# A row-number map carried as the 129th float of each gathered row

## What is computed

```python
agg = jax.ops.segment_sum(x[src], dst, num_segments=N_NODES)
h = x + agg
h = jnp.maximum(h @ wa + ba, 0.0)
return h @ wb + bb
```

## Time and profile before

| | us |
|---|---|
| median of 2 runs | 3564.31 |
| lowest and highest of them | 3557.01, 3571.61 |
| span of the profiled execution, first to last instruction | 5308.1 |
| opening, in the profiled execution | 0 to 49.3 |
| dense layers, in it | 49.3 to about 1465 |
| sums of the first layer, in it | about 1465 to 1965 |

### The profile page before, as it was taken

One profiled execution on the slowest core, in us unless ns is written; L12 is line 12 of the kernel. 1 busy time (PEld: TensorE's weight loads), 2 busy tenths in 40 slices (PEclk: granted clock), 3 DMA queues, 4 the chain that ended last, 5 costly groups with the idle time before them and its releaser, 6 DMA issues. The chain is left out here.

```text
span 5308.1 us, 70155 instructions
## 1 busy us (share of the span) xinstructions
PE 3134.5 (59%) x18625; PEld 2527.0 (48%) x18625; DVE 2677.8 (50%) x8976; ACT 2356.1 (44%) x6177; POOL 2154.2 (41%) x2226
## 2 busy tenths in 40 slices
PE   1110107999867779868756403997029970178864
PEld 1000006777644445534446403996029870177764
DVE  1000008999943346559846301775006860199875
ACT  0000007999812224447735302775017750188765
POOL 6777760000045555546366473001740017500366
PEclk7555559999967777779967656987559975598555
DMA  2200004444434433425556423765227752276542
GB/s 77 56 9 8 18 9 140 174 172 170 164 117 127 119 87 108 112 90 168 164 155 200 142 63 104 225 196 163 62 72 233 220 177 61 58 245 232 169 125 82
DMA packets 430539, 673.46 MB, mean 127 GB/s; under 512 B 81411, under 2 KB 168086, under 8 KB 430252
## 3 DMA queue, kind: packets, MB, share of 16 engines
q1 hardware_dynamic: 354764, 558.83, 32.6%
q0 software_dynamic: 70464, 108.96, 8.9%
q10 hardware_dynamic: 5024, 2.30, 0.2%
HBM read 378.46 MB, written 295.50 MB: 127 GB/s over the span
## 5 line engine op out<-in xcount | busy, mean ns | idle before, releaser
L647 POOL DMA_INDIRECT msgs<-t_gat,row_i x600 | 574.3, 957 | 1081.6 <-POOLq L157 895.1
L664 POOL DMA_INDIRECT dg_g_ring<-in_x,dst_i x200 | 192.2, 961 | 860.5 <-DVE g_xb L1222 782.9
L2229 ACT ACTIVATE t_nnt<-t_p_nt,cxt 128x512 f32<-128x512 f32 x294 | 200.4, 682 | 756.0 <-remote 265.3
L1754 PE MATMUL t_p_q<-mean_col,t_nsq 128*128 128x1 f32 x2352 | 332.6, 263 | 273.2 <-issue 243.0
L1754 PEld LDWEIGHTS t_p_q<-mean_col,t_nsq 128*128 128x128 f32 x2352 | 342.9, 224 | 280.8 <-issue 280.8
L2023 POOL DMA_INDIRECT out_rows<-t_x,own_i x200 | 204.4, 1022 | 491.1 <-ACT t_x L2279 437.9
L2109 PE MATMUL t_p_nt<-ident,t_nh 128*128 128x128 f32 x1176 | 217.7, 316 | 309.3 <-issue 176.1
L1747 PE MATMUL t_p_nh<-wx,t_nnt 128*128 128x132 f32 x1568 | 265.1, 320 | 178.9 <-issue 156.1
L800 PE MATMUL de_p_o<-wc,de_hh 128*128 128x128 f32 x1568 | 225.8, 289 | 151.5 <-DVE de_r L948 124.3
L2109 PEld LDWEIGHTS t_p_nt<-ident,t_nh 128*128 128x128 f32 x1176 | 158.1, 163 | 328.9 <-issue 231.4
L1747 PEld LDWEIGHTS t_p_nh<-wx,t_nnt 128*128 128x128 f32 x1568 | 228.4, 221 | 179.9 <-issue 179.4
(11 more groups left out here) (405 smaller groups left out, 9434.7 us busy)
## 6 DMA issues: line engine op xcount, KB each, us to landing
t_nh<-t_gat SPq DMA_DIRECT2D x294, 264.0 KB
t_gat<-t_nhn SPq DMA_DIRECT2D x196, 264.0 KB
t_x<-de_x SPq DMA_DIRECT2D x196, 256.0 KB
t_ah<-t_gat SPq DMA_DIRECT2D x150, 264.0 KB
t_x<-t_x SPq DMA_DIRECT2D x148, 256.0 KB
t_gat<-t_ahn SPq DMA_DIRECT2D x100, 264.0 KB
t_gat<-de_h SPq DMA_DIRECT2D x98, 264.0 KB
de_x<-in_x SPq DMA_DIRECT2D x97, 256.0 KB
```

Source lines behind the costliest of these rows:

```text
L647: self.nc.gpsimd.indirect_dma_start(out=self.msgs[:, c, 0:width], out_offset=None, in_=table, in_offset=bass.IndirectOffsetOnAxis(ap=idx[: ...
L664: nc.gpsimd.indirect_dma_start(out=ring[:, u, j, :], out_offset=None, in_=a["x"], in_offset=bass.IndirectOffsetOnAxis(ap=self.dst_i[:, i * ...
L1754: last = self.nc.tensor.matmul(p_q[:, j:j + 1], sq[:, j * D:(j + 1) * D], self.mean_col[:], start=True, stop=True)
L2229: nc.scalar.activation(nnt[:, g % 2], p_nt[:], ACT.Identity, bias=bias).then_inc(act_nt, 1)
```

## The change

There is no `t_where` any more. A new table `t_xw` in DRAM has NPAD rows of MW = 129 floats: a node's row of `x` and, as 129th float, the number of the row where the node is right. Slot numbers are now held as floats.

- In the opening POOL first writes the nodes' own row numbers (`node_row`, in the memory of `deg`). ACT, after its 26 loads, issues 7 DMAs that write these into the 129th place of every row, 128 x 56 single floats each, and then 16 that copy `x` from DRAM into the 129-float rows, 3125 rows of 512 bytes each. Two semaphores that outlive the block count their landings.
- The opening prepares target numbers (`dst_i`) before source numbers, and the resident gathers into `msgs` now bring target rows. They read `x` as before.
- POOL waits for the fills, scatters the slot numbers (into `t_xw` now), gathers the last LATE = 8 chunks, waits for the copies and the scatters, and then brings source rows of 129 floats through the ring. The reads of the map and the two copies of zeroes are gone.
- In the first layer's sums the ring's rows go to the scan and the resident rows to the addition. DVE copies the 129th floats of each group into `row_i`, one small copy for each of the 50 groups.

```diff
     def load(act):
         for dst, src in loads:
             act.dma_start(dst, src).then_inc(loaded, 16)
+        act.wait_ge(self.nodes_told, 1)
+        t = NPAD // 128
+        rows = self.xw[0:NPAD, D:MW].rearrange("(p t) o -> p (t o)", p=128)
+        for n in range(FILLS):
+            part = slice(n * t // FILLS, (n + 1) * t // FILLS)
+            act.dma_start(rows[:, part], self.node_row[:, part]).then_inc(self.map_filled, 16)
+        for n in range(COPIES):
+            part = slice(n * N // COPIES, (n + 1) * N // COPIES)
+            act.dma_start(self.xw[part, 0:D], a["x"][part, :]).then_inc(self.x_copied, 16)
...
-        self.resident_gather(self.src_i, a["x"], D, got, range(FIRST, CHUNKS))
+        self.resident_gather(self.dst_i, a["x"], D, self.got, range(FIRST, CHUNKS - LATE))
+        pool.wait_ge(self.map_filled, 16 * FILLS)
         for c in range(CHUNKS):
             nc.gpsimd.indirect_dma_start(
-                out=self.where, out_offset=bass.IndirectOffsetOnAxis(ap=self.put_i[:, c:c + 1], axis=0),
+                out=self.places, out_offset=bass.IndirectOffsetOnAxis(ap=self.put_i[:, c:c + 1], axis=0),
                 in_=self.slot_id[:, c:c + 1], in_offset=None).then_inc(mapped, 16)
-        for i in range(UN):
+        self.resident_gather(self.dst_i, a["x"], D, self.got, range(CHUNKS - LATE, CHUNKS))
+        pool.wait_ge(self.x_copied, 16 * COPIES)
+        pool.wait_ge(mapped, 16 * CHUNKS)
+        for i in range(AG):
             rows(i)
-        pool.wait_ge(got, 16 * CHUNKS)
-        for n in range(2):
-            pool.dma_start(self.msgs[0:1, n * ROWP:(n + 1) * ROWP, 0:D],
-                           self.t4[SLOTS:SLOTS + ROWP, :].rearrange("(o c) f -> o c f", o=1)).then_inc(self.zeroed, 16)
-        pool.wait_ge(mapped, 16 * CHUNKS)
-        ahead = CHUNKS - (AG - UN)
-        for c in range(ahead):
-            look(c)
-        for i in range(UN, AG):
-            rows(i)
-            look(ahead + i - UN)
-        pool.wait_ge(self.map_taken, 16 * CHUNKS)
...
+                    if live(k, u, 1, AG):
+                        dve.wait_ge(arrived[v], 16 * G4 * (k + (0 if u < 1 else 1)))
+                        nc.vector.tensor_copy(self.row_i[:, bass.ds((i - 1) * G4, G4)], xs[:, v, :, D]).then_inc(s["dve_row"], 1)
```

More of the change, by code:

```diff
@@ L35 @@
 XW = D + 4
+MW = D + 1
+COPIES = 16
+FILLS = 7
 RE = 2 * CE
@@ L178, in allocate @@
         self.got = ctx.enter_context(nc.semaphore("got"))
+        self.x_copied = ctx.enter_context(nc.semaphore("x_copied"))
+        self.map_filled = ctx.enter_context(nc.semaphore("map_filled"))
         def sb(name, shape, dt=F32):
@@ L315, in store @@
             sp.dma_start(self.t4[SLOTS:SLOTS + 128, :], spread[:, 3, :]).then_inc(stored, 16)
+            for n in range(N, NPAD, 128):
+                m = min(NPAD, n + 128)
+                sp.dma_start(self.xw[n:m, 0:D], spread[0:m - n, 3, :]).then_inc(stored, 16)
             sp.wait_ge(loaded, 16 * len(loads))
-            sp.wait_ge(stored, 16)
+            sp.wait_ge(stored, 48)
         def fill(pool):
+            nc.gpsimd.iota(self.node_row, pattern=[[1, NPAD // 128]], base=SLOTS, channel_multiplier=NPAD // 128,
+                           allow_small_or_imprecise_dtypes=True).then_inc(self.nodes_told, 1)
             nc.gpsimd.memset(self.ident[:], 0.0).then_inc(ready, 1)
@@ L416, in turn @@
             last.then_inc(columns, 1)
-        return load, store, fill, fold, turn, stored, ready
+        return load, store, fill, fold, turn, ready
     def segments_parts(self, sb, ps, sem):
@@ L451, in segments_parts, with store @@
                                 a[name][whole * RE:E].rearrange("(o k) -> o k", o=1)))
[L452 to L455, removed]
+        dst_loaded, dst_row, dst_turned, dst_ready = (sem(n) for n in ("dst_loaded", "dst_row", "dst_turned", "dst_ready"))
+        n_loads = len(other_loads) + 1
         def load(sp):
             sp.wait_ge(cleared, 4)
-            for dst, src in src_loads:
-                sp.dma_start(dst, src).then_inc(src_loaded, 16)
-            for dst, src in dst_loads + other_loads:
+            for dst, src in dst_loads:
+                sp.dma_start(dst, src).then_inc(dst_loaded, 16)
+            for dst, src in other_loads:
                 sp.dma_start(dst, src).then_inc(loaded, 16)
             sp.dma_start(wcomp[:], a["L1_gnn_w_comp"].rearrange("(o r) b -> o r b", o=1).to_broadcast([128, 8, 4])).then_inc(loaded, 16)
[L465 to L469, removed]
+        def store(sp):
+            sp.wait_ge(told, 7)
+            sp.dma_start(self.unplaced, self.slot_id[:]).then_inc(gone, 16)
             sp.wait_ge(flagged, 1)
@@ L505, in find @@
             of = lambda n: p[n][:, 0:CHUNKS].rearrange("q (j p) -> q j p", j=2)
-            dve.wait_ge(src_loaded, 32)
+            dve.wait_ge(dst_loaded, 16 * len(dst_loads))
             dve.wait_ge(cleared, 4)
[L508 to L511, removed]
+            after(nc.vector.tensor_copy(dstf[:], dst_raw[:]))
+            cur = halves(dstf[:, 1:RE + 1])
+            nc.vector.tensor_scalar(halves(row[:, 1])[:, :, 1:128], cur, float(N - 1), None, ALU.min).then_inc(dst_row, 1)
+            dve.wait_ge(dst_turned, 1)
+            nc.vector.tensor_copy(both(self.dst_i[:]), of(1)).then_inc(dst_ready, 1)
             dve.wait_ge(loaded, 16 * n_loads)
-            dve.wait_ge(told, 8)
-            after(nc.vector.tensor_copy(dstf[:], dst_raw[:]))
+            dve.wait_ge(told, 7)
             after(nc.vector.memset(dstf[0:1, 0:1], -1.0))
-            cur = halves(dstf[:, 1:RE + 1])
             at = lambda t: halves(t[:])[:, :, 1:128]
@@ L583, in turn @@
             idp = self.ident[0:ROWP, 0:ROWP]
-            for n in range(1, 6):
+            for n in (0, 2, 3, 4, 5):
                 for j in range(2):
```

99 lines of the change are left out of this document (50 added, 49 removed).

## The result

The changed kernel takes 3804.02 us (two runs, 3798.41 and 3809.64), before it was 3564.31: a ratio of 1.0688, 95% interval 1.0644 to 1.0733, or +239.7 us. The forecast was 3880, in a range of 3480 to 4040. The profiled execution of the changed kernel is one of the timed ones: its own time is 3809.64 us, its span 3807.8.

A forecast was written before the change was run, and what follows sets the result against it. Dense work, bounded by DVE, and POOL's queue were taken to reach the sums almost together, with POOL setting the sums' pace. +376 us (opening) and -60 (sums) on 3564.3 gave 3880 us, range 3480 to 4040.

The forecast's parts named there:

- Dense work beside POOL: Ahead of the sums: in timed runs dense work goes on beside POOL at its own pace, 6.85 us a group.
- ACT is held until its queue has drained: In the opening: 100,176 pieces hold ACT, so the next block begins at 425 us instead of 49.3, +376 us.
- Five engines for 3125 rows: In the opening: each 3125-row copy runs on 5 engines, its largest divisor up to 16; 149 rows a us.
- Drain of the fills: On ACT's queue in the opening: 50,176 pieces of 4 bytes drain in 75 us, between 38 and 105.
- Drain of the copies: On ACT's queue in the opening: 50,000 rows of 512 bytes drain in 335 us, between 263 and 750.
- the sum: Whole kernel: +376 us in the opening and -60 in the sums, +316 on 3564.3, giving 3880 us.
- Rival 2: In the opening: ACT held, but copies use 16 engines and take 105 us; total 3650 us; chance 0.10.
- POOL perhaps 30 us later: Ahead of the sums: dense work ends near 760 us, POOL near 790; removing 154 reads saves at most 30 us.
- -60 us for the reads: In the sums: removing the reads of the map saves 60 us, between 0 and 93.
- POOL's pace of 6.3 us a group: In the sums: POOL needs 290 us, 6.3 us a group, and PE is near that pace as well.
- The 50 small copies on DVE: In the sums: copies of about 171 ns each, 8.6 us in all, hidden beside DVE's other work.

The follow-up runs named there:

- e9: The kernel before plus only 16 copies of x on ACT's queue, 3136-row pieces, into a plain unread 128-float table, no fills: 3628.82 us in one execution.
- e3: The kernel before with the change's fills and copies added on ACT's queue, into a table nobody reads: 5659.94 us against 5330.86, ratio 1.0596.
- e11: The changed kernel with its copies issued by SP as 98 pieces beside dense groups, fills still on ACT: 3537.64 us, 0.9913 of the kernel before.
- e2: The changed kernel with its 16 copies cut into 15 pieces of 3128 rows and one of 3080: 0.9929 of the kernel before.
- e8: The changed kernel with 154 reads of single numbers added again, behind the ring's first four groups: 3835.27 us, 1.0694 of the kernel before.
- e7: The changed kernel with 46 reads of single numbers added again, one behind each ring group 4 to 49: 3900.66 us, 1.0872 of the kernel before.
- e10: The changed kernel with its 200 scatters sent into a compact table of 4-byte places that nobody reads: 3848.97 us, 1.0799 of the kernel before.
- e1: The changed kernel with its 16 copies cut into 15 pieces of 3136 rows and one of 2960: 0.9917 of the kernel before.
- e5: The changed kernel as it is, in a session of the slower kind: 5371.46 us against 5277.32 for the kernel before, 1.0181.

## Why the prediction was right, and where not

- **Dense work beside POOL** was inferred from 1744 us between span and median. Right for the timed runs, as the profile of e9 shows of the kernel before; the pace of a group, given as 6.85 us, measured 83.4 / 12 = 6.95.
- **ACT is held until its queue has drained.** Right, though it rested on one issue of 1.89 us: ACT is the last at the barrier by 318 us, alone this cost 329 us (e3), and without the copies on it the change is a gain (e11).
- **Five engines for 3125 rows.** Right: 80 closing packets, and 8 engines shortened the copies from 295 to 206 us (e2).
- **Drain of the fills**, 75 us: measured 60.5, and 66 to 73 in the runs. **Drain of the copies**, 335 us at 33 ns a row and engine: measured 295 at 29.6. The opening grew by 324.6 us instead of 376, and these 51 are most of the 76 by which the forecast lay above the result; the other 25 are give-back that the sum left out (last point). Both errors point the same way, so no luck brought the number near.
- **Rival 2's price**, 105 us for sixteen engines, was wrong: 193 us. The rate of 477 rows a us was read from loads into SBUF and does not hold from DRAM to DRAM, where 259 was the most.
- **"POOL perhaps 30 us later"** was wrong. Dense work came out too short, since its ramp was left out: the first group's last transposes come 51 us into the block. In the kernel before itself POOL's queue is through 718 us into the block, with 738 reckoned (e9: 801.07 + 0.94 - 83.78), and the first scan comes at 777, so POOL was ahead of it and not behind; the 154 reads were worth 3 us at most in the trace (e8).
- **-60 us for the reads** was right in size, and it is the 46 within the sums alone (57 to 63 us, e9 and e7). PE was taken to be near POOL's pace of 6.3 us a group; it is busy 219.94 of 220 us, but at 4.96 a group. The 50 small copies on DVE took 170 ns each, as forecast, and lie beside it.
- **Left out: what the scatters do to others.** I gave them POOL's time only. Into a table of 4 bytes a node they slow dense work by 31 us (e9, e10), which the new layout saves. 57 + 31 = 88 is what the second block of e9 shows (89).

## What to carry to other kernels

A DMA issue is not free because its engine has nothing to compute: here the issuer waited while its queue drained, and the barrier behind it made everybody wait. So count the pieces of a transfer and not only its bytes (25.6 MB in 50,000 pieces held ACT for 295 us, in pieces of 33 KB for 11), and spread a large one in small portions over a queue with room, as e11 does, whose 98 copies cost some 8 us. What takes instructions from a queue is worth something only in the stage where that queue sets the pace: here 46 of 200 in the faster kind of session. And where numbers are scattered to can cost others more than the scatter costs its issuer.

## What the hardware showed unexpectedly

- Copies of 512-byte rows from DRAM to DRAM, into rows 516 bytes apart: 169, 242 and 259 rows a us on 5, 8 and 16 engines (changed kernel, e2, e1). Where both sides lie in one piece, packets of 33 KB ran at 314 GB/s, 335 with the other queues (e9, 50 to 80 us).
- POOL's DRAIN at the end of the opening, behind 24 gathers, ended 2.5 us after the last of their issues before, and 44 us after it with such copies beside it (e9).
- 4-byte scatters into a table of 4 bytes a node raised other transfers' packets from 78 to 184 ns (e9) and 173 (e10), though the scatters' own share was about 3%. That the spacing of the places does it (or the table's size, which goes with it) is shown by e10 against the changed kernel; by what mechanism is open.
- Beside POOL's gathers dense work ran at full pace (rows above) or nearly stood still, on the same kernel. In e5 two successive groups came 100 us apart while POOL issued, where they take 6.9 when POOL is idle:

```profile
518.58 0.69 DVE L954 TENSOR_TENSOR de_r<-de_p_o,de_x 128x512 f32<-128x512 f32 x1 [55.58 <-remote]
...
619.38 0.69 DVE L954 TENSOR_TENSOR de_r<-de_p_o,de_x 128x512 f32<-128x512 f32 x1 [54.67 <-remote]
```

One chip number showed both (e5 and e10), so it is not the chip alone. What decides between the two is open, and no run tried it.
